# Six attention layers on one core: V leaves the projections, probabilities times tokens instead, masks and exps moved between engines, shifts by transfers

## The chip, the cores and the metric

One Trainium2 chip, one of its cores. The metric is the device time of one execution in microseconds. An execution is a single launch; all weights and inputs come from device memory and the result goes back to it. Five engines work beside each other, each with its own instruction queue in program order: TensorE (PE in the profile, PEld its weight loads), VectorE (DVE), ScalarE (ACT), GpSimd (POOL) and SyncE (SP, which issues the transfers here). They meet at semaphores only.

## The reference

The input x has 4 batches of 512 tokens of 128 numbers. Everything is float32. Two parts follow each other.

```
# part 1: attention with relative positions, 16 heads of 8, on layernorm(x)
score = ((q + u) @ k^T + relative_shift((q + v) @ pos^T)) / sqrt(8)
x1 = x + softmax(score) @ val @ Wo + bo
# part 2: x = layernorm(x1), then six layers, each
x' = shift_tokens(x)                 # second half of the features comes from the token before
q, k, v = split(x' @ Wqkv)           # 16 heads of 64
q, k = rotary(l2norm(q) * qs), rotary(l2norm(k) * ks)
# windows of 32 queries see the 64 keys of their own and the previous window, masked
x = x + softmax(8 q k^T, masked) @ v @ Wo
xn = layernorm(shift_tokens(x)) * g + b
a, gate = split(xn @ W1 + b1)
x = x + (a * gelu(gate)) @ W2 + b2
# at the end: x + x1
```

## The kernel before

**Part 1** (`relative_attention`, L817) runs through 128 rounds. Score rows go out to a scratch array in device memory and come back shifted by one; the transfers of this keep the memory busy. At its end, x is loaded once more (L963), POOL adds `bo` (L1194), and the block closes with a meeting of all engines.

**Part 2** (`local_layers`, L45) works on tiles of 128 tokens: 4 tiles are one batch and are called a group here, 16 tiles a layer, 96 tiles the whole. It begins with the last projection of part 1 for all four batches (L595 to L605) and their norm. Then each engine walks the same list of periods (`PERIODS`, L161), one tile per period. Several tiles are in flight: in period n, TensorE projects K and V of tile n and Q of tile n+1, turns (transposes) q and k of tile n-1, makes the scores of tile n-1, turns the probabilities of n-2, multiplies them with V for n-3 and projects the output of n-3 (the order by hand is L606 to L629; the others are L296 for POOL, L410 for ACT, L765 for DVE). An engine never looks ahead in its list, so one wait holds all that stands behind it.

Of one tile: two halves of 512 columns each make K, V or Q (L463). DVE multiplies q and k by the two rotary tables (`rotate`, L643, four instructions of 1024 numbers), ACT squares them (L317), DVE sums the squares by head (L652), POOL makes the inverse norms by three Newton steps for this tile (L243 to L266), adds the rotary halves (L240, four instructions) and scales q and k (L275). TensorE turns them (L473), ACT copies them out (L335, L344). The mask enters the scores as a bf16 matmul (L491); 64 small matmuls add q times k (L499). DVE takes the maximum (L658) and subtracts it (L666), ACT takes all exps in one instruction (L363), DVE sums, inverts and divides (L674, L681, L687), TensorE turns the probabilities (L510), ACT copies them (L369). SP spreads v over `vwin` by 16 transfers a tile (L177 to L189), 64 small matmuls make the head outputs (L529), ACT copies them (L376), 8 matmuls with Wo follow (L541), DVE adds to x (L694).

Once a group, after the fourth tile's addition: TensorE shifts the tokens by two matmuls with a shifted identity (`shift`, L545), DVE takes the statistics of the layernorm (L696), POOL the deviation (L277), ACT normalises in eight instructions of 64 numbers with a scale and a bias by partition (L393), TensorE turns (L561), three pairs of W1 matmuls (`hidden`, L569), three gelus on ACT (L402, with a table load before them and one before the next exp), three gates on DVE (L721), W2 (L579) and the addition (L730). PSUM (the matmuls' output memory) has eight banks; `ROOM` (L118) says which kind of result uses which, and `take` (L437) makes TensorE wait until the former user of a bank has been read.

## Time and profile before

| | us |
|---|---|
| three timed runs: median (lowest to highest) | 2131.49 (2127.36 to 2133.46) |
| the profiled execution, its own time | 2129.15 |
| its span in the profile | 2127.4 |
| part 1, until the meeting of the engines | about 442 |

| engine | busy share of the span |
|---|---|
| PE | 95% |
| POOL | 71% |
| DVE | 70% |
| ACT | 60% |

Busy shares are means over both parts. A row of the timeline gives the start and the length of a run of equal instructions; matmul passes overlap their neighbours by about 0.2 us of modelled drain, so the cost of a step is read from its start to the start of the next step. A float32 matmul shows as two passes, a transpose as one. In a row of waits or lines, "<-" names what ended the idle time. The granted clock of TensorE has two levels, shown as 1.00 (2.4 GHz) and 0.50 (1.2 GHz).

### The profile page before, as it was taken

To read this page: it belongs to the slowest core of one execution; us is meant where nothing else is said; L and a number is where in the kernel's file an instruction comes from. 1 tells how busy PE (TensorE), PEld (TensorE's weight loads), DVE (VectorE), ACT (ScalarE), POOL (GpSimd) and SP (SyncE) were. 2 spreads that over 40 slices of the span, in tenths; PEclk is the share of its full clock that TensorE was granted. 3 is DMA by queue.
4 is the path that set the end of the run, shared out by engine and by line. 5 is a ranking of instruction groups with operands and counts; after the bars stand their busy time and mean duration, and the time that the engine had idled before them with its cause. 6 is when DMAs were issued, how large, how long until landed. Compare 5 with 4: busy or idle time off the path is not lost.

```text
span 2127.4 us, 84221 instructions
## 1 busy us (share of the span) xinstructions
PE 2025.2 (95%) x35763; PEld 1357.7 (64%) x35763; DVE 1498.2 (70%) x2267; ACT 1285.3 (60%) x1844; POOL 1521.0 (71%) x2315
## 2 busy tenths in 40 slices
PE   6899998979999999999999999999999999999997
PEld 2555555545666667766676666766676666766665
DVE  3445454458877788778777788777787788777873
ACT  4676767535655666566655566566665666566653
POOL 4344444468888788777887788778887788877880
PEclk9999999989999999999999999999999999999998
DMA  6999999922224222242232322224222242222221
GB/s 201 331 347 354 340 352 351 328 73 59 65 67 115 63 66 70 62 114 62 63 73 63 111 68 66 63 64 112 67 72 64 61 118 62 67 63 63 66 70 41
DMA packets 121588, 261.51 MB, mean 123 GB/s; under 512 B 29140, under 2 KB 36224, under 8 KB 120448
## 3 DMA queue, kind: packets, MB, share of 16 engines
q1 hardware_dynamic: 121216, 256.13, 41.3%
q8 instruction: 285, 4.67, 0.9%
q14 instruction: 87, 0.71, 0.1%
HBM read 87.06 MB, written 68.29 MB: 73 GB/s over the span
## 4 chain that ended last, share of the span: by engine, by line
PE 72%; POOL 2%; DVE 2%; issue 1%; ACT 1%; POOLq 0%; DVEq 0%; ACTq 0%
PE ring L463 24%; PE ring L529 9%; PE ring L473 8%; PE yps L541 8%; PE ring L499 7%; PE ring L569 5%; PE ring L510 4%; PE tpose L579 3%; PE ring L491 1%; DVE turned L643 1%; PE tpose L551 1%; PE tpose L561 1%; POOL ropes L229 0%; POOL roped L275 0%; PE yps L454 0%
## 5 line engine op out<-in xcount | busy, mean ns | idle before, releaser
L643 DVE TENSOR_TENSOR turned<-ring,ropes 128x1024 f32<-128x1024 f32 x384 | 452.2, 1220 | 301.4 <-PE ring L463 301.4
L240 POOL TENSOR_TENSOR roped<-turned 128x512 f32<-128x512 f32 x384 | 522.1, 1385 | 171.8 <-PE ring L473 171.0
L463 PE MATMUL ring<-wqkv,xT 128*128 128x512 f32 x1152 | 565.2, 614 | 6.1 <-ACT xT L328 4.9
L275 POOL TENSOR_TENSOR roped<-roped,rnorm 128x1024 f32<-128x1024 f32 x192 | 361.2, 1902 | 7.5
L1188 POOL TENSOR_SCALAR less<-less,lowest 128x512 f32<-128x512 f32 x256 | 174.4, 692 | 216.1 <-DVE lowest L1141 216.1
L1141 DVE CUSTOM_DVE_ANT_0 less<-ps_b,shifted 128x512 f32<-128x512 f32 x256 | 166.7, 689 | 211.7 <-issue 89.5
L463 PEld LDWEIGHTS ring<-wqkv,xT 128*128 128x128 f32 x1152 | 197.6, 191 | 161.0 <-issue 149.3
L369 ACT COPY pT<-ring 128x1024 f32<-128x1024 f32 x96 | 97.1, 1012 | 305.3 <-PE ring L510 305.3
L529 PEld LDWEIGHTS ring<-pT,vwin 64*64 64x64 f32 x12288 | 198.3, 134 | 51.4 <-issue 51.1
L317 ACT ACTIVATE squares<-ring 128x1024 f32<-128x1024 f32 x192 | 197.2, 1027 | 55.0 <-DVE turned L643 54.9
L529 PE MATMUL ring<-pT,vwin 64*64 64x32 f32 x12288 | 219.4, 220 | 4.3 <-issue 2.6
L652 DVE TENSOR_REDUCE ss<-squares 128x16 f32<-128x1024 f32 x192 | 221.3, 1184 | 1.1 <-ACT squares L317 0.9
L473 PEld LDWEIGHTS ring<-ident,roped 128*128 128x128 f32 x1536 | 175.1, 142 | 72.1 <-issue 40.8
L473 PE MATMUL ring<-ident,roped 128*128 128x128 f32 x1536 | 205.4, 277 | 10.7 <-POOL roped L275 5.1
L499 PEld LDWEIGHTS ring<-kT,qT 64*32 64x32 f32 x12288 | 140.6, 105 | 98.3 <-issue 96.2
L541 PE MATMUL yps<-wo,oT 128*128 128x128 f32 x1536 | 187.4, 275 | 1.2 <-ACT oT L376 1.1
L972 PE MATMUL ps_b<-posm,qvT 32*128 32x512 f32 x512 | 147.1, 662 | 41.4 <-DVE lowest L1141 39.0
L541 PEld LDWEIGHTS yps<-wo,oT 128*128 128x128 f32 x1536 | 179.1, 192 | 1.6 <-ACT oT L376 1.6
L499 PE MATMUL ring<-kT,qT 64*32 64x64 f32 x12288 | 174.4, 224 | 2.3 <-issue 2.2
L1048 PEld LDWEIGHTS ps_b<-ident,less 128*128 128x128 f32 x1024 | 111.4, 142 | 93.6 <-POOL less L1188 76.9
L344 ACT COPY kT<-ring 128x1024 f32<-128x1024 f32 x96 | 97.0, 1011 | 101.7 <-PE ring L473 101.7
L1241 ACT ACTIVATE pT_a<-ps_b 128x512 f32<-128x512 f32 x256 | 141.5, 614 | 24.8 <-PE ps_b L1048 24.6
(134 smaller groups left out, 3242.0 us busy)
## 6 DMA issues: line engine op xcount, KB each, us to landing
vwin<-v SPq DMA_DIRECT2D x1536, 64.0 KB, 2.0
shifted<-scratch_w SPq DMA_DIRECT2D x64, 1024.0 KB, 12.0
scratch_w<-wrows SPq DMA_DIRECT2D x48, 1026.0 KB, 10.2
scratch_w<-x SPq DMA_DIRECT2D x16, 1026.0 KB, 9.9
wqkv<-in_l_wqkv SPq DMA_DIRECT2D x6, 1536.0 KB, 6.7
wo<-in_l_wo SPq DMA_DIRECT2D x6, 512.0 KB
w<-in_l_w SPq DMA_DIRECT2D x6, 342.0 KB
w<-in_l_w SPq DMA_DIRECT2D x6, 171.0 KB
```

The lines of the kernel that those rows point to most:

```text
L240: nc.gpsimd.tensor_tensor(halves[2][:, :, side, :], halves[0][:, :, side, :], halves[1][:, :, 1 - side, :], ALU.add).then_inc(s[name + "_a ...
L275: nc.gpsimd.tensor_tensor(whole, whole, norm, ALU.mult).then_inc(s[name + "_roped"], 1)
L317: nc.scalar.activation(squares[:, n, :], ring[:, room(name.upper()), :, :].rearrange("p b c -> p (b c)"), ACT.Square).then_inc(s[name + "_ ...
L463: last = nc.tensor.matmul(out[:, half, :], xT[:, t % SEQT * P:(t % SEQT + 1) * P], wqkv[:, layer_of(t), at + half * 512:at + (half + 1) * ...
L473: last = nc.tensor.transpose(out[:, j * P:(j + 1) * P], roped[:, n, j * P:(j + 1) * P], ident[:, :])
L499: last = nc.tensor.matmul(out[W * win:W * win + W, r, j * W2:(j + 1) * W2], qT[rows, j, W * win:W * win + W], kT[rows, j, at:at + W2], sta ...
L529: last = nc.tensor.matmul(out[a * DH:(a + 1) * DH, r, at:at + W], vwin[rows, p, win, j * DH:(j + 1) * DH], pT[rows, j, W * win:W * win + W ...
L541: last = nc.tensor.matmul(out[:, 0:D], oT[:, j % 2, j // 2, :], wo[:, layer_of(t), j, :], start=j == 0, stop=j == PAIRS - 1)
L643: ins = nc.vector.tensor_tensor(turned[:, n, part, :].rearrange("p (h d) -> p h d", d=DH), heads, table, ALU.mult)
L652: nc.vector.tensor_reduce(ss[:, n * HEADS:(n + 1) * HEADS], squares[:, n, :].rearrange("p (h d) -> p h d", d=DH), AX.X, ALU.add).then_inc( ...
L1141: nc.vector.tensor_tensor_reduce(less[:, c % 2, k, :], ps[:, 2 + k, :], shifted[:, c // 2 % NR, k, c % 2, :], -SCALE0, HIGHEST, ALU.add, A ...
L1188: nc.gpsimd.tensor_scalar(less[:, c % 2, k, :], less[:, c % 2, k, :], -1.0, lowest[:, c % 2, k:k + 1], ALU.mult, ALU.add).then_inc(s["scal ...
```

## The change

- V is no longer projected, copied, spread or multiplied. Instead x itself is laid out by SP in `xwin` (seven transfers a group), for each query window the 64 tokens that it may see, already shifted. TensorE multiplies these tokens by the probabilities of all 16 heads (`attend`: 8 matmuls of 32 rows, 128 columns and 512 moving columns, in four row groups and four banks), ACT copies the result by two instructions, and 16 matmuls with `wvo` give the output. `wvo` is Wv times Wo by head, made once a layer by 8 transposes and 16 matmuls.
- The mask is added by DVE as it reads the scores out (`take_scores`); the maximum is taken from that copy; q is no longer scaled by its norm, the exps take it as their scale, so they are 16 instructions of 64 numbers, one a head, each with a scale and a bias by partition.
- POOL divides the probabilities and does the Newton steps for two tiles at once; the scaling of q is gone. DVE turns the probabilities in blocks of 32 by 32 (`turn_p`) in place of TensorE and the ACT copy.
- The shift of the tokens before the second norm is done by two transfers into `xs` (`shift`, now SP's): one of 127 partitions, one of a single partition. DVE's `statistics` waits for both.
- All orders of the periods are new, with one more to two more tiles in flight; K and Q of one tile are projected in one period. FFN steps of a group sit in periods of their own: with n modulo 4, `statistics` and the W2 matmuls in 1, `turn_xn` in 2, two `hidden` at the end of 3, the third at the start of 0.
- In part 1, the output projection, the residual and the norm of batches 0 to 2 are done between the rounds (`FINISH`), x stays in its buffer, and the first layer's Wqkv is loaded before the block closes. Part 2 begins with batch 3's projection alone.

The core of the diff, new lines:

```diff
+        ROOM = {"AT": 3, "AP": 4, "XT": 3, "K": 2, "Q": 0, "QT": 1, "KT": 1, "S": 0, "O0": 1, "O1": 2, "Y": 4, "XN": 3, "H0": 0, "H1": 1, "H2": 2, "F": 3, "WV": 1, "M0": 1, "M1": 1}
...
+            def windows(g):
+                p, half = g % 2, D // 2
+                tiles = x[:, g % BATCH * SEQT:(g % BATCH + 1) * SEQT, :]
+                if g == BATCH - 1:
+                    sp.wait_ge(s["normed"], SEQT)
+                elif g >= BATCH:
+                    sp.wait_ge(s["x_done"], g - BATCH + 1)
+                at_least(sp, s["o_made"], SEQT * (g - 1))
+                low, high, up = slice(0, half), slice(half, D), W + 1
+                moves = [(xwin[:, p, :, 1, low], tiles[:, :, low]),
+                         (xwin[1:P, p, :, 1, high], tiles[0:P - 1, :, high]),
+                         (xwin[0:1, p, 1:SEQT, 1, high], tiles[P - 1:P, 0:SEQT - 1, high]),
+                         (xwin[W:P, p, :, 0, low], tiles[0:P - W, :, low]),
+                         (xwin[0:W, p, 1:SEQT, 0, low], tiles[P - W:P, 0:SEQT - 1, low]),
+                         (xwin[up:P, p, :, 0, high], tiles[0:P - up, :, high]),
+                         (xwin[0:up, p, 1:SEQT, 0, high], tiles[P - up:P, 0:SEQT - 1, high])]
+                for dst, src in moves:
+                    sp.dma_start(dst, src).then_inc(windows_in[p], 16)
+            def shift(g):
+                if lives(g):
+                    tiles = x[:, g % BATCH * SEQT:(g % BATCH + 1) * SEQT, D // 2:D]
+                    sp.wait_ge(s["y_added"], SEQT * (g + 1))
+                    at_least(sp, s["xn_made"], g)
+                    sp.dma_start(xs[1:P, :, :], tiles[0:P - 1, :, :]).then_inc(s["shifted"], 16)
+                    sp.dma_start(xs[0:1, 1:SEQT, :], tiles[P - 1:P, 0:SEQT - 1, :]).then_inc(s["shifted"], 16)
...
+            for g in range(GROUPS + 2):
+                if g < GROUPS:
+                    windows(g)
+                shift(g - 2)
+                if g % BATCH == 2 and g // BATCH + 1 < DEPTH:
+                    load_layer(g // BATCH + 1)
...
+                if live(t) and t % 2 == 0:
+                    m = t // 2
+                    sums, of_pair, part = (y.rearrange("p t h -> p (t h)") for y in (ss[:, m % 2, :, :], rnorm[:, m % 2, :, :],
+                                                                                      newton[:, :, :]))
+                    pool.wait_ge(s["q_summed"], t + 2)
+                    pool.wait_ge(s["k_summed"], t + 2)
...
+            def divide(t):
+                if live(t):
+                    pool.wait_ge(s["rinv_made"], t + 1)
+                    whole = probs[:, t % 2, :, :, :].rearrange("p r j k -> p (r j) k")
+                    nc.gpsimd.tensor_tensor(whole, whole, rinv[:, :, :].rearrange("p r j -> p (r j)").unsqueeze(2).broadcast_to(
+                        [P, HEADS, W2]), ALU.mult).then_inc(s["p_normed"], 1)
...
+                add_b2(group_of(n - 13))
+                add(1, n - 1)
+                divide(n - 4)
                 norms(n - 2)
...
+                    act.wait_ge(s["ebias_made"], t + 1)
+                    for r in range(2):
+                        for j in range(PAIRS):
+                            h = 2 * j + r
+                            of_head = probs[:, t % 2, r, j, :]
+                            ins = nc.scalar.activation(of_head, of_head, ACT.Exp, scale=norm_of(t)[:, h:h + 1],
+                                                       bias=ebias[:, t % 2, r, j:j + 1])
+                    ins.then_inc(s["exped"], 1)
+            def copy_o(t, half):
+                if live(t):
+                    act.wait_ge(s["o_made"], t + 1)
+                    at_least(act, s["y_made"], t - 1)
+                    nc.scalar.copy(xpT[:, t % 2, :, 2 * half:2 * half + 2, :].rearrange("p h w q -> p w h q"),
+                                   pair("O" + str(half)).rearrange("p w (h q) -> p w h q", q=W)
+                                   ).then_inc(s["o_copied" + str(half)], 1)
...
+                copy_xn(group_of(n - 11))
+                copy_q(n - 2)
+                copy_next_wvo(n - 2)
+                gelus(group_of(n - 12), 2)
+                gelus(group_of(n - 12), 1)
+                gelus(group_of(n - 12), 0)
+                exps(n - 3)
+                square(1, n)
+                copy_k(n - 2)
+                copy_x(n + 1)
                 square(0, n)
+                copy_o(n - 4, 0)
+                copy_o(n - 4, 1)
+                normalise(group_of(n - 9))
...
+            def attend(t):
+                if live(t):
+                    p = t // SEQT % 2
+                    pe.wait_ge(s["p_turned"], t + 1)
+                    pe.wait_ge(windows_in[p], WINDOWS * (t // SEQT // 2 + 1))
+                    take("O0", t)
+                    take("O1", t)
+                    for half in (1, 0):
+                        for win in range(WT):
+                            rows = slice(W * win, W * win + W)
+                            last = nc.tensor.matmul(pair("O" + str(win // 2))[:, win % 2, :], xwin[rows, p, t % SEQT, half, :],
+                                                    pT[rows, t % 2, :, half, :], start=half == 1, stop=half == 0)
+                    last.then_inc(s["o_made"], 1)
+            def project_out(t):
+                if live(t):
+                    for half in range(2):
+                        pe.wait_ge(s["o_copied" + str(half)], t + 1)
+                        pe.wait_ge(s["wvo_copied" + str(half)], t // (SEQT * BATCH) + 1)
+                    out = take("Y", t)
+                    for h in range(HEADS):
+                        last = nc.tensor.matmul(out[:, 0:D], xpT[:, t % 2, h, :, :].rearrange("p w q -> p (w q)"),
+                                                wvo[:, layer_of(t), h // PAIRS, h % PAIRS, :], start=h == 0,
+                                                stop=h == HEADS - 1)
+                    last.then_inc(s["y_made"], 1)
...
+                        at = 2 * INNER + j * P
+                        last = nc.tensor.transpose(out[:, j * P:(j + 1) * P], wqkv[layer % 2][:, at:at + P], ident[:, :])
...
+                            rows, at = slice(r * DH, (r + 1) * DH), a * PAIRS // 2 + j
+                            last = nc.tensor.matmul(out[:, r, j * D:(j + 1) * D], wvT[rows, at, :], wo[layer % 2][rows, at, :],
...
+                hidden(group_of(n - 12), 0)
+                turn_x(n + 1)
                 project("K", n)
+                project("Q", n)
+                turn_qk(1, n - 2)
+                project_out(n - 5)
+                attend(n - 4)
+                scores(n - 2, 0)
+                scores(n - 2, 1)
+                project_ffn(group_of(n - 13))
+                turn_xn(group_of(n - 10))
                 turn_qk(0, n - 1)
+                next_wvo(n - 1)
+                hidden(group_of(n - 11), 2)
+                hidden(group_of(n - 11), 1)
...
+                    seen = mask[:, 1 if t % SEQT == 0 else 0, :].unsqueeze(1).broadcast_to([P, HEADS, W2])
+                    nc.vector.scalar_tensor_tensor(probs[:, t % 2, :, :, :].rearrange("p r j k -> p (r j) k"),
+                                                   pair("S").rearrange("p r (j k) -> p (r j) k", k=W2), QK_SCALE, seen,
+                                                   ALU.mult, ALU.add).then_inc(s["scores_taken"], 1)
...
+                    nc.vector.scalar_tensor_tensor(ebias[:, t % 2, :, :], smax[:, :, :], -1.0, norm, ALU.mult, ALU.mult
+                                                   ).then_inc(s["ebias_made"], 1)
...
+            def turn_p(t):
+                if live(t):
+                    dve.wait_ge(s["p_normed"], t + 1)
+                    at_least(dve, s["o_made"], t - 1)
+                    nc.vector.transpose(pT[:, t % 2, :, :, :].rearrange("p h s q -> p (h s q)"),
+                                        probs[:, t % 2, :, :, :].rearrange("p r j k -> p (r j k)")).then_inc(s["p_turned"], 1)
...
-                    dve.wait_ge(s["shifted"], g + 1)
+                    dve.wait_ge(s["shifted"], 32 * (g + 1))
...
+                sum_squares(1, n - 1)
+                sum_squares(0, n - 1)
+                offsets(group_of(n - 10))
+                add_y(n - 6)
+                take_scores(n - 3)
+                take_max(n - 3)
+                exp_bias(n - 3)
+                gate(group_of(n - 12), 1)
+                add_ffn(group_of(n - 14))
+                gate(group_of(n - 12), 2)
+                statistics(group_of(n - 9))
+                turn_p(n - 4)
+                gate(group_of(n - 12), 0)
+                rotate(1, n)
                 rotate(0, n)
+                sum_probs(n - 3)
+                invert(n - 3)
+                if n == 8:
+                    first_norm()
...
+                    sp.wait_ge(s["c_taken"], 2 * 2 * ROUNDS // BATCH)
+                    sp.dma_start(kept["early"][:, 0:3 * INNER], layers["wqkv"][0]).then_inc(kept["qkv0_loaded"], 16)
...
+                        if c in FINISH:
+                            b = FINISH[c]
+                            pe.wait_ge(s["o_done"], max(turned_units, VARS * (b + 1)))
+                            for i in range(STEPS):
+                                last = nc.tensor.transpose(ps[:, 7, i * P:(i + 1) * P], attn[:, b * STEPS + i, :], ident[:, :])
+                            last.then_inc(s["a_turned"], 1)
...
+            FINISH = {85: 0, 93: 1, 101: 2}
```

## Rows read from the trace of the kernel before

**Rows 1.** The page, the chain that ended last (whole span)

```profile
PE ring L463 24%; PE ring L529 9%; PE ring L473 8%; PE yps L541 8%; PE ring L499 7%; PE ring L569 5%; PE ring L510 4%; PE tpose L579 3%; PE ring L491 1%; DVE turned L643 1%; PE tpose L551 1%; PE tpose L561 1%; POOL ropes L229 0%; POOL roped L275 0%; PE yps L454 0%
```

**Rows 2.** Busy time by windows, part 2: window, length, busy us by engine, clock, DMA

```profile
514.50:2053.80 1539.30, 1530.23 (x29817) 1056.11 (x29817) 1209.41 (x1469) 938.40 (x1217) 1244.89 (x1897) 1.00 0.29 74
```

**Rows 3.** Timeline of TensorE in two periods: start, length, what

```profile
1516.62 1.14 PE L529 MATMUL ring<-pT,vwin 64*64 64x32 f32 x64
1517.68 1.98 PE L463 MATMUL ring<-wqkv,xT 128*128 128x512 f32 x4
1519.60 0.41 PE L491 MATMUL ring<-bias,identb 32*32 32x512 bf16 x8
1519.94 0.96 PE L499 MATMUL ring<-kT,qT 64*32 64x64 f32 x64
...
1523.53 1.09 PE L510 MATMUL ring<-ident,probs 128*128 128x128 f32 x8
1524.46 0.60 PE L561 MATMUL tpose<-ident,xn 128*128 128x128 f32 x4
1524.90 1.95 PE L541 MATMUL yps<-wo,oT 128*128 128x128 f32 x16
1526.68 1.88 PE L463 MATMUL ring<-wqkv,xT 128*128 128x512 f32 x4
...
1529.53 5.31 PE L569 MATMUL ring<-xnT,w 128*114 128x512 f32 x12
...
1550.44 2.94 PE L579 MATMUL tpose<-w,hT 114*128 114x128 f32 x24
```

**Rows 4.** Timeline of TensorE in part 1, four row groups at once

```profile
23.08 1.31 PE L972 MATMUL ps_b<-posm,qvT 32*128 32x512 f32 x8
24.32 0.67 PE L990 MATMUL ps_b<-ident,x 128*128 128x128 f32 x4
```

**Rows 5.** Timeline of ACT, two of the eight instructions of normalise

```profile
1521.81 0.43 ACT L393 ACTIVATE xn<-x,offset,rstd 128x64 f32<-128x64 f32 x1
1522.14 0.39 ACT L393 ACTIVATE xn<-tpose,offset,rstd 128x64 f32<-128x64 f32 x1
```

**Rows 6.** Lines, 700 to 2100 us: busy us, mean ns | idle before

```profile
L240 POOL TENSOR_TENSOR roped<-turned 128x512 f32<-128x512 f32 x323 | 442.5, 1395 | 151.6 <-PE ring L473 151.5
L643 DVE TENSOR_TENSOR turned<-ring,ropes 128x1024 f32<-128x1024 f32 x320 | 377.0, 1220 | 256.5 <-PE ring L463 256.5
L275 POOL TENSOR_TENSOR roped<-roped,rnorm 128x1024 f32<-128x1024 f32 x162 | 304.8, 1902 | 6.3
...
L666 DVE TENSOR_TENSOR probs<-ring,smax 128x1024 f32<-128x1024 f32 x82 | 100.4, 1224 | 2.8
...
L344 ACT COPY kT<-ring 128x1024 f32<-128x1024 f32 x82 | 82.9, 1011 | 90.6 <-PE ring L473 90.6
...
L402 ACT ACTIVATE gelu<-ring,b 114x512 f32<-114x512 f32 x63 | 41.1, 685 | 9.2 <-PE ring L569 7.9 <-DVE hT L721 0.9
...
L402 ACT ACT_TABLE_LOAD x21 | 26.9, 1283 | 0.4
...
L701 DVE BATCH_NORM_STATS2 stats<-x 128x6 f32<-128x64 f32 x84 | 18.1, 216 | 13.4 <-PE tpose L553 13.4
```

**Rows 7.** Transfers, 700 to 2000 us: packets, MB, share of 16 engines; the vwin issues

```profile
q1 hardware_dynamic: 63141, 91.30, 28.0%
...
vwin<-v SPq DMA_DIRECT2D x1226, 64.0 KB, 2.0
```

**Rows 8.** Window at the end of a layer's load (its w2 and b1 have 114 partitions)

```profile
1196.50:1197.50 1.00, 0.79 (x51) 0.68 (x44) 1.00 (x2) 0.79 (x1) 1.00 (x1) 1.00 0.39 155
```

**Rows 9.** Windows at the end of the output's store (128 partitions)

```profile
2126.25:2126.50 0.25, 0.00 (x0) 0.00 (x0) 0.00 (x0) 0.00 (x0) 0.00 (x0) 0.50 0.95 270
2126.50:2126.75 0.25, 0.00 (x0) 0.00 (x0) 0.00 (x0) 0.00 (x0) 0.00 (x0) 0.50 0.11 29
```

**Rows 10.** Timeline of TensorE after a long wait, start of part 2

```profile
462.65 7.47 PE L463 MATMUL ring<-wqkv,xT 128*128 128x512 f32 x12 [4.93 <-ACT xT L328]
```

More of the change, by code:

```diff
@@ L556, in turn_xn, with next_wvo @@
+            def next_wvo(t):
+                step, layer = t % (SEQT * BATCH), t // (SEQT * BATCH) + 1
+                if t >= TURN_WV - SEQT * BATCH:
+                    if step == TURN_WV:
+                        turn_wv(layer)
+                    for a in range(2):
+                        if step == TURN_WV + 1 + a:
+                            make_wvo(layer, a)
             def turn_xn(g):
```

653 lines of the change are left out of this document (280 added, 373 removed).

## The prediction

> **What bounds the kernel now.** I read three views in this order. The chain of waits first [rows 1]: nearly every entry is TensorE, and only with lines of the second part. Then the busy time by windows [rows 2]: from the K projection of tile 4 (514.5 us) to that of tile 95 (2053.8 us) TensorE is busy 1530 of 1539 us, at full clock, so a period is TensorE's own sum. 91 periods in 1539.3 us are 16.92 us each, 67.7 us for a group of four. In that time DVE is busy 13.3 us a period (1209.41/91), ACT 10.3, POOL 13.7. Third the timeline of TensorE [rows 3], for what each step costs from its start to the next start: one of K, Q, V 1.92 us (1517.68 to 1519.60), the mask 0.34, the turn of the probabilities 0.93, the turn of xn 0.44, the output projection 1.78, half of the old attend 1.06 (1516.62 to 1517.68); the whole hidden about 5.4 and the W2 matmuls about 2.8, each its length less the drain. What holds for this kernel: microseconds taken from TensorE's list are gained as long as no other engine gets in its way. The reader is to see how thin the reserve of the others becomes.
>
> **TensorE's list.** Gone per tile: V 1.92, mask 0.34, turn of the probabilities 0.93, attend 2 x 1.06 = 2.12; together 5.31, or 21.2 a group, and the shift, 0.9 a group (1% of the span in the chain [rows 1] over 24 groups). Added per tile: eight more output matmuls, so 1.78 again, and the new attend. That one is not in this trace in its form, but its kind is: eight passes of 32 rows and 512 columns, on four row groups, take 1.24 us from start to start [rows 4], where passes of 128 rows take 0.48 each (1.92/4). Attend has sixteen such passes. Twice 1.24 is the high end with four abreast, half of the serial 16 x 0.48 = 7.7 is two abreast, 7.7 is none; the low end is 16/4 x 0.43 = 1.7. I take 2.2, near the row. So 4 x (1.78 + 2.2) = 15.9 a group. Wv times Wo is 8 transposes (0.93) and 32 half-height passes (between 1 and 4 us) a layer: 0.7 a group. Sum: 67.7 - 21.2 - 0.9 + 15.9 + 0.7 = 62.2 us a group, 15.5 a period.
>
> **ACT.** Two copies of 1.01 go (V, probabilities), one of 1.01 comes (attend's result in two halves) [rows 6]. The exps become 16 instructions of 64 numbers with scale and bias by partition. Normalise has that form: 0.33 us from start to start, 0.43 long [rows 5]. So 16 x 0.34 = 5.4 us, for 1.06 before; if they did not overlap, 6.9. ACT goes from 10.3 to 13.6 us a period, 15.1 at the worst: below TensorE's, but now long stretches of it are on the way to the next TensorE step. **DVE** keeps its sum: the division goes to POOL, the turn of the probabilities comes. It has no row; it moves 1024 numbers, for which rows of DVE give 1.22 [rows 6], a second pass would make 2.4; I take 1.2. The mask and the factor 8 ride on the copy that was there (1.22). **POOL** loses one scaling (1.90) and gains the division (1.90 by the same form [rows 6]); its fifteen small instructions now serve two tiles, which saves some 2 us a period. DVE stays near 13.3, POOL near 11.7, both under 15.5. Each can still be late once in a while; 0 to 1 us a group, taken as 0.
>
> **Where the order makes TensorE wait.** Each period has one loop that all engines share: scores of a tile done, then DVE's copy 1.22, maximum 1.2, bias 0.15; ACT's exps 5.4, square of k 0.92, copy of k 0.91; then TensorE may attend, since the copy of k frees attend's bank, and after it makes the next scores. With the hand-overs that is 10.1 us before attend. In the same time TensorE has turn q 0.93, x 0.12, K and Q 3.8, turn k 0.93, output 3.56: 9.3 us. By n modulo 4: in 1 it waits 10.1 - 9.3 = 0.8. In 2 the W2 matmuls of the period before make it 12.1: no wait. In 3, with turn_xn, 9.7: 0.4. In 0 the hidden matmuls make it 14.7; but the last of them ends at 6.4, then gelu 0.65, table load 1.28 [rows 6], exps, square and copy end at 15.8: 1.1. Together 2.3, so 64.5 us a group, 16.1 a period.
>
> **The new transfer.** This is the step that decides. TensorE's shift becomes two transfers, and DVE's `statistics` waits for them in the very period (n modulo 4 is 1) in which DVE adds the group's last y. Queued behind this wait on DVE are turn_p (attend needs it) and both rotates (ACT's square of k needs the first, so does the copy of k behind it in ACT's list). The addition is over about 0.9 us before the scores are done; DVE has 2.6 us of other work after that, so a landing up to 3.6 us after the addition costs nothing.
>
> How long does it take? It moves 127 partitions of 4 x 256 bytes, 130 KB. The 64 KB transfers of v land in 2.0 us [rows 7], and all transfers of this stretch ran at 91.30 MB / (0.28 x 16 x 1300 us) = 15.7 KB per us and DMA engine [rows 7]. Spread over 16 engines the shift would land after 2.0 + 0.3; on one engine after 2.0 - 0.3 + 8.3 = 10.0. Which is it? The load of a layer ends with a tail [rows 8]: for a whole microsecond only 39% of the DMA engines' time is used, while the store over 128 partitions ends within a quarter of a microsecond, from 95% to 11% [rows 9]. The load is the one case here with transfers of 114 partitions (w2, 171 KB, and b1), which is no multiple of 16: 155 KB moved in the tail at 39%, about what six engines would do that have all of w2 to themselves (6/16 = 0.375). So transfers over such a count use fewer engines, as many as divide it, and 127 has no divisor but 1. I take one engine: 10.0 us and 0.1 for SP's wake. The low end is 9.1 (the bulk of the store moves 270/16/0.95 = 17.8 KB per us and engine [rows 9], so 7.3 in place of 8.3), the high end 14 if pieces of 256 bytes cost more than their share.
>
> The Trainium skill states this outright, in "DMA: Bandwidth & Descriptors", section "Why a DMA increments its semaphore by 16 and not by 1": the number of engines is the largest up to 16 that divides the slowest dimension of both sides, and 127 partitions all go to one. The tail in the trace agrees with it for 114 (six engines). By the opposite reading, 16 engines, the sum would be the first rival's.
>
> Landing is then 10.1 - 0.9 = 9.2 us after the scores. Behind it: statistics 8 x 0.13 + 0.4 = 1.5 (overlapping, 0.22 each [rows 6]), turn_p 1.2, rotate k 2.3, square 0.92, copy 0.91: attend at 16.0 and not at 10.1, so 5.9 us more a group. In this wait TensorE stands idle for more than 6 us. After an idle 4.93 us at the start of part 2 twelve passes took 7.47 instead of 5.8 us [rows 10], since the clock was at its lower level. I add 2.1 for attend, scores and the W2 matmuls after it (between 0 and 4). 64.5 + 5.9 + 2.1 = 72.5 us a group, 18.1 a period. The windows' seven transfers have the same trouble (127, 95 and 33 partitions), but are issued some four periods ahead of their use, so they cost nothing.
>
> **Start and end.** Part 1 is bound by transfers and keeps its 442 us; the three finished batches lie in TensorE's gaps there. Part 2 starts with one batch and loaded weights, and its first periods lack the later steps: K of tile 5 comes some 20 us earlier (an estimate: five periods of about 11 us for five of 15 to 17). At the end, from K of tile 95 on, one more to two more periods drain, and one shift is bare: before 73.6 us (2127.4 less 2053.8), after about 92. Net -2 us (-10 without the slow transfer).
>
> **Sum.** 90 periods x (18.1 - 16.92) = +106, less 2: 2129 (the profiled execution's own time, 2 us over its span and 2 us under the median of the runs) + 104 = 2233 us.
>
> **Rivals.**
> First: the transfer is spread or otherwise in time (below 3.6 us). For it: the 64 KB transfers land in 2.0 us. Against it: the tail. Then 16.1 a period: 90 x (16.1 - 16.92) = -74, -10: 2045 us, faster. The point from which it decides is the landing: up to 3.6 us free, equal to the kernel before at about 7 us (3.2 us a group over 64.5, with little clock loss), slower beyond.
> Second: the transfer is in time, but the exps do not overlap (0.43 each, 1.5 us more in three of four periods, 4.5 a group): 17.25 a period, 2129 + 30 - 10 = 2149, slower by 1%. Against it: the eight of normalise overlap [rows 5].
> Third: attend runs two abreast (3.9 instead of 2.2, 6.8 a group) on top of the slow transfer; its wait then hides none of it: 90 x 1.7 more, 2386 us. Against it: [rows 4].
> That the change does less than it says: if the clock stays up after the wait and DVE catches up part of it, 68 to 70 a group: 2135 to 2180, the likeliest case's lower part.
>
> **How the numbers follow.** Likeliest 0.66, first rival 0.22, second 0.05, third 0.04, the rest 0.03. Time: 2233. The likeliest case's own range is 2130 to 2320 (landing 8 to 12 us, clock 0 to 4 us a group, loops +-1.5 us a group, which is +-34 us). The range over all takes in the first rival: 2030 to 2320. Within 0.3% of before (about 6 us, what a measurement can tell from nothing) lies little: 0.05. Faster: the first rival and the lowest part of the likeliest, 0.27. Slower: 0.68.
>
> **What would show it.** In the profile after: a landing of xs near 10 us; idle time of DVE before the statistics (bn_stats), released by that transfer, some 7 us x 24; rows of TensorE's attend with 16 passes in about 2.2 us; exps 0.34 us from start to start; a granted clock below 1.00 once a group; DMA share well under today's 0.29. If the transfer lands under 4 us, my step on its engines is wrong and the time is near 2045. If it lands at 10 and the kernel is still faster, the slack that I gave DVE before the statistics is wrong. If part 2 has 16.1 us or less in all other periods, the sums of the engines were right.

## The result and the profile after

The changed kernel takes 2238.27 us (median; 2234.71 to 2242.56), the kernel before 2132.47 beside it: ratio 1.0497, 95% interval 1.0464 to 1.0531. It is slower by 106 us. The profiled execution has a span of 2232.9 us.

The page after, part 1 (busy time) and part 4 (the chain that ended last, by engine and line):

```profile
PE 1887.8 (85%) x24771; PEld 1270.8 (57%) x24771; DVE 1523.8 (68%) x2363; ACT 1610.8 (72%) x3204; POOL 1305.9 (58%) x1639
...
ACT 26%; PE 26%; DVE 9%; DMA 9%; issue 8%; POOL 1%; SPq 1%; ACTq 0%; DVEq 0%; POOLq 0%
```

The chain of before is nearly all TensorE [rows 1]. Now TensorE and ACT have a quarter each, and 9% of the span, 200 us, is one kind of transfer. The busy time by windows, from K of tile 5 to K of tile 95, as [rows 2]:

```profile
526.40:2125.60 1599.20, 1374.15 (x19136) 957.21 (x19135) 1223.59 (x1548) 1231.38 (x2478) 1034.36 (x1245) 0.96 0.08 19
```

TensorE is busy 1374 of 1599 us: 15.3 us in a period of 17.77. Its list did get shorter (16.8 before), and 2.5 us a period of waiting have come in. The DMA share fell from 0.29 to 0.08, the clock from 1.00 to 0.96. The next fences show one group around its last addition of y. DVE:

```profile
1516.01 0.28 DVE L743 TENSOR_TENSOR x<-yps,x 128x128 f32<-128x128 f32 x1
1517.05 1.23 DVE L697 SCALAR_TENSOR_TENSOR probs<-ring,mask 128x1024 f32<-128x1024 f32 x1 [0.76 <-PE ring L539]
1518.31 1.22 DVE L704 TENSOR_REDUCE smax<-probs 128x16 f32<-128x1024 f32 x1
1519.56 1.14 DVE L715 SCALAR_TENSOR_TENSOR ebias<-smax,rnorm 128x16 f32<-128x16 f32 x1
1525.60 0.23 DVE L750 BATCH_NORM_STATS2 stats<-x 128x6 f32<-128x64 f32 x1 [4.90 <-DMA xs<-x]
```

SP's queue in the same stretch, the two issues of the shift:

```profile
1516.32 0.70 SPq L224 DMA_DIRECT2D xs<-x  x1
1517.07 6.50 SPq L225 DMA_DIRECT2D xs<-x  x1
```

The addition ends at 1516.29, the statistics start at 1525.60: the shift lands after 9.3 us. Windows while it runs (length, busy us by engine, clock, DMA share, GB/s):

```profile
1519.00:1520.00 1.00, 0.77 (x13) 0.80 (x15) 0.97 (x2) 0.08 (x1) 1.00 (x2) 1.00 0.08 17
1521.00:1522.00 1.00, 1.00 (x4) 0.49 (x3) 0.00 (x0) 1.00 (x3) 0.00 (x0) 1.00 0.08 18
```

A share of 0.08 of the DMA engines' time is used, at 17 to 18 GB/s. The rate is that of one engine in [rows 9] (17.8 KB per us), and kernel 5 below, with 122 partitions, has twice the share and nearly twice the rate: one engine carries the 127 KB. The divisor rule that the prediction took from [rows 8] holds here. What waits behind it, on ACT and then TensorE:

```profile
1530.55 1.02 ACT L357 ACTIVATE squares<-ring 128x1024 f32<-128x1024 f32 x1 [3.81 <-DVE turned L678]
1531.47 1.01 ACT L383 COPY kT<-ring 128x1024 f32<-128x1024 f32 x1
```

```profile
1513.60 2.00 PE L556 MATMUL ring<-pT,xwin 32*128 32x512 f32 x16 [0.72 <-ACT kT L383]
1515.53 1.48 PE L539 MATMUL ring<-kT,qT 64*32 64x64 f32 x128
...
1524.79 3.74 PE L568 MATMUL yps<-wvo,xpT 128*128 128x128 f32 x32
1532.73 3.51 PE L556 MATMUL ring<-pT,xwin 32*128 32x512 f32 x16 [4.20 <-ACT kT L383]
```

Follow the chain by its start times: the statistics start behind the landing at 1525.60, DVE's rotate of K ends about 1530.5, ACT squares and copies, TensorE attends at 1532.73. The same attend takes 2.00 us at 1513.60 and 3.51 after the wait; the windows say why (clock is the number before the DMA share):

```profile
1532.80:1536.10 3.30, 3.30 (x16) 1.21 (x16) 3.27 (x4) 1.14 (x2) 2.55 (x2) 0.54 0.01 2
1536.30:1537.50 1.20, 1.20 (x128) 1.19 (x123) 0.36 (x3) 1.20 (x2) 0.78 (x3) 1.00 0.00 0
```

After 4.2 us idle the granted clock is 0.54, near its lower level (1.2 GHz), as in [rows 10], where it is 0.50 from 462.7 to 466 us; for the scores it is back at 1.00. The sums over the run, from the waits (total, times, longest):

```profile
PE ring L556 <- ACT kT L383: 177.7, 91, 8.8
...
DVE stats L750 <- DMA xs<-x: 120.4, 24, 9.3
```

### The profile page after: what moved, and what is told of

The parts are those of the page before. It is cut to its first block, busy times and chain, and to the rows that moved or that the text cites. A ratio compares the mean times of both kernels' runs of the same rounds, so it can differ in the third digit from the quotient of the medians.

```text
span 2232.9 us, 61471 instructions
## 1 busy us (share of the span) xinstructions
PE 1887.8 (85%) x24771; PEld 1270.8 (57%) x24771; DVE 1523.8 (68%) x2363; ACT 1610.8 (72%) x3204; POOL 1305.9 (58%) x1639
## 4 chain that ended last, share of the span: by engine, by line
ACT 26%; PE 26%; DVE 9%; DMA 9%; issue 8%; POOL 1%; SPq 1%; ACTq 0%; DVEq 0%; POOLq 0%
ACT probs L394 15%; DMA xs<-x 9%; PE ring L556 8%; PE ring L618 6%; PE ring L539 5%; ACT kT L383 4%; DVE turned L678 3%; PE tpose L629 3%; ACT squares L357 3%; PE ring L522 2%; ACT qT L374 1%; DVE probs L697 1%; DVE smax L704 1%; ACT L394 1%; DVE stats L750 1%
## 5 line engine op out<-in xcount | busy, mean ns | idle before, releaser
L394 ACT ACTIVATE probs<-probs,ebias,rnorm 128x64 f32<-128x64 f32 x1536 | 519.7, 428 | 41.9 <-DVE ebias L715 41.5
L556 PE MATMUL ring<-pT,xwin 32*128 32x512 f32 x1536 | 232.7, 726 | 181.8 <-ACT kT L383 177.7
L568 PE MATMUL yps<-wvo,xpT 128*128 128x128 f32 x3072 | 358.8, 275 | 1.6 <-DVE x L743 1.6
L568 PEld LDWEIGHTS yps<-wvo,xpT 128*128 128x128 f32 x3072 | 350.7, 192 | 2.3 <-issue 2.3
L277 POOL TENSOR_TENSOR roped_k<-turned 128x512 f32<-128x512 f32 x192 | 240.2, 1274 | 186.9 <-DVE turned L678 100.9
L277 POOL TENSOR_TENSOR roped_q<-turned 128x512 f32<-128x512 f32 x192 | 239.5, 1270 | 77.7 <-PE ring L522 77.7
L403 ACT COPY xpT<-ring 128x1024 f32<-128x1024 f32 x192 | 185.1, 1016 | 126.9 <-PE ring L556 126.9
L319 POOL TENSOR_TENSOR probs<-probs,rinv 128x1024 f32<-128x1024 f32 x96 | 182.6, 1902 | 125.3 <-DVE rinv L729 125.3
L313 POOL TENSOR_TENSOR roped_k<-roped_k,rnorm 128x1024 f32<-128x1024 f32 x96 | 183.1, 1907 | 3.8
L509 PE MATMUL ring<-wqkv,xT 128*128 128x512 f32 x384 | 175.2, 599 | 5.9 <-DVE gelu L768 5.9
L539 PE MATMUL ring<-kT,qT 64*32 64x64 f32 x12288 | 154.3, 237 | 22.5 <-issue 14.3
```

Of the source, the lines that this page charges most:

```text
L277: nc.gpsimd.tensor_tensor(halves[2][:, :, side, :], halves[0][:, :, side, :], halves[1][:, :, 1 - side, :], ALU.add).then_inc(s[name + "_a ...
L313: nc.gpsimd.tensor_tensor(whole, whole, norm, ALU.mult).then_inc(s["k_roped"], 1)
L319: nc.gpsimd.tensor_tensor(whole, whole, rinv[:, :, :].rearrange("p r j -> p (r j)").unsqueeze(2).broadcast_to([P, HEADS, W2]), ALU.mult).t ...
L394: ins = nc.scalar.activation(of_head, of_head, ACT.Exp, scale=norm_of(t)[:, h:h + 1], bias=ebias[:, t % 2, r, j:j + 1])
L403: nc.scalar.copy(xpT[:, t % 2, :, 2 * half:2 * half + 2, :].rearrange("p h w q -> p w h q"), pair("O" + str(half)).rearrange("p w (h q) -> ...
L509: last = nc.tensor.matmul(out[:, half, :], xT[:, t % SEQT * P:(t % SEQT + 1) * P], wqkv[layer_of(t)][:, at + half * 512:at + (half + 1) * ...
```

## The experiments

All times are medians (kernel 9 has a single execution); ratios are to the kernel before on the same chip, with their 95% intervals. For each kernel the time is cut at two marks of TensorE's timeline, K of tile 5 and K of tile 95; these 90 periods are "a period", the rest up to the end of the span is "tail". "n1" is the mean distance from the start of one scores block to the next where the later one lies in a period with n modulo 4 = 1, the period in which the shift is awaited (21 of them, n = 13 to 93). There is no kernel 8.

```
kernel                          time     K(5) at  period   tail   n1
before                          2132     529.2    16.94    73.6   -
after                           2238     526.4    17.77   107.3   20.9
1  shift in 112+15              2123     528.9    16.44   102.2   15.2
2  windows cut, shift whole     2251     534.3    17.82   108.9   20.9
3  both cut                     2117     529.4    16.50   102.7   15.5
4  statistics late, shift whole 2191     534.6    17.14   110.4   15.4
5  shift in 122+5               2151     532.3    16.77   105.2   16.6
6  3, one exp (prices its form) 2037     528.5    15.67    94.2   14.3
7  3, exps split in two         2192     533.2    17.32    97.3   16.9
10 7, square of Q ahead too       2318     533.7    18.62   103.7   18.4
9  3, attend by window          2119     531.9    16.45   104.7   15.5
11 3, norm by DVE, no maximum   2049     527.3    15.77    94.5   14.1
12 11, all transfers whole      2179     530.5    17.19   100.7   20.5
```

**1. The shift cut at 112 partitions** (seven times 16, and 15). Theory A: the one-engine transfer. Rival B: something else in the new loop. Code is shortened in all edits shown: the increments and the counts of the waits, which follow the number of transfers, are left out.

```
-  sp.dma_start(xs[1:P, :, :], tiles[0:P - 1, :, :])
+  sp.dma_start(xs[1:113, :, :], tiles[0:112, :, :])
+  sp.dma_start(xs[113:P, :, :], tiles[112:P - 1, :, :])
```

> The changed kernel with its token shift of 127 partitions cut into two transfers, of 112 and of 15 partitions; all else as it is. Theory A (one DMA engine carries all of the 127 partitions, DVE's statistics wait for it and hold turn_p and the rotates): the landing falls from 9.3 us after the addition to about 2.5 to 3.5 us, the wait of the statistics (120 us in all) goes to under 10 us, and with the clock's drop behind it 6 to 7.5 us a group go: 2055 to 2095 us, ratio to before 0.965 to 0.98. Theory B (the loop over scores, sixteen exps and attend is the bound, the transfer only fills a wait that is there anyway): at most 20 us less than 2238.

Measured 2122.94, ratio 0.9945 (0.9925 to 0.9965). 115 us come back, and the kernel is 0.5% faster than before. DVE's wait for xs is gone from the periods: it reaches the statistics 4.3 us after the addition, and the data lie there. (In kernels 7 and 10 it is there sooner and waits until 3.4 us after the addition: that is the landing of 112 + 15.) SP's second issue, 6.50 us with the whole shift, now takes 0.86 (timeline of SP):

```profile
1381.58 0.65 SPq L224 DMA_DIRECT2D xs<-x  x1
1382.28 0.86 SPq L225 DMA_DIRECT2D xs<-x  x1
1383.19 0.72 SPq L226 DMA_DIRECT2D xs<-x  x1
```

B, which allowed 20 us, is out as the main cause of the loss. But A had 2055 to 2095: more was left besides the transfer than I worked out, and what it was stands in the section on the prediction.

**2. The windows' transfers cut, the shift whole**, and **3. both cut.** C: TensorE's stray stops come from the seven slow window transfers.

```
-  (xwin[1:P, p, :, 1, high], tiles[0:P - 1, :, high]),
+  (xwin[1:113, p, :, 1, high], tiles[0:112, :, high]),
+  (xwin[113:P, p, :, 1, high], tiles[112:P - 1, :, high]),
   (the same for the pieces of 95 and 33 partitions: 80 + 15, 32 + 1)
```

> The changed kernel with only the seven window transfers cut so that no part of more than one partition has a count with few divisors (127 into 112 and 15, 95 into 80 and 15, 33 into 32 and 1); the shift stays whole. Theory A says that the windows are ahead of their use: the time stays within 10 us of 2238. Theory C (TensorE's own instructions arrive by the same DMA engines, and the scores stop for 1.8 us a group while the windows crowd one engine): that stop goes, 40 to 70 us less, 2170 to 2195.

> Both cuts at once. Theory A alone: as the shift's cut alone, 2055 to 2095. A and C together: some 45 us less than that, 2010 to 2050; the prediction's first rival gave 2045.

Measured 2250.7 (1.0562, 1.0532 to 1.0592) and 2116.68 (0.9931, 0.9908 to 0.9954). C falls. Alone, cutting the windows costs some 12 us, little over the 10 that A allowed. Of the 14 us between the two traces 8 lie before K of tile 5, where kernel 4, whose windows are whole, is as late; what they come from is not shown. With the shift cut the intervals of kernels 1 and 3 overlap. As the prediction said, the slowness of these transfers costs nothing: no gain comes from cutting them.

**4. The statistics moved behind the inversion in DVE's period**, transfers whole: the turn of the probabilities and the rotates no longer stand behind the wait.

```
                 statistics(group_of(n - 9))     (taken out before turn_p)
                 ...
                 invert(n - 3)
+                statistics(group_of(n - 9))
```

> The changed kernel with the slow transfer kept, but DVE's statistics moved behind the rotates, the sum and the inverse of the same period, so that nothing of that period stands behind the wait. Theory A: DVE waits little, attend is on time; 5 to 7 us a group go, 2070 to 2120 us. A rival (the wait only moves to ACT's normalise and to the copy of q behind it): 1 to 3 us a group go, 2165 to 2215. Theory B: no change.

Measured 2190.56, ratio 1.0274 (1.0257 to 1.0292): the time that the rival gave, but not by its way. n1 is 15.4, as with the cut transfer, but the period with n modulo 4 = 2 went from 16.4 to 19.1. From the waits of this kernel:

```profile
POOL rstd L326 <- DVE meanvar L754: 230.2, 24, 27.1
DVE turned L678 <- POOL roped_q L277: 103.0, 26, 7.2
...
PE ring L522 <- POOL roped_k L313: 58.1, 25, 5.8
```

The first is 175.8 us in the kernel after, the second 16.4. The third is 8.5. POOL's small `deviations` stands in its list ahead of the additions and the scaling of K of the next period. The wait was handed in good part from DVE's queue to POOL's. ACT's normalise, to which the rival had it move, waited once in the whole run, 15.7 us, as in the kernel after. The move cured 48 of 115 us.

**5. The shift cut at 122 partitions** (two times 61, and 5): two engines.

> The shift is cut at 122 partitions (2 times 61) and 5, so that by the rule of divisors two DMA engines move the large part and five the small one. Theory (the landing after the addition decides, and the engines are counted by divisors): the transfer takes about 2 + 7.5/2 = 5.7 us instead of 9.25. That is some 2 us over the 3.6 us that DVE has free, so 1.5 to 2.5 us a group are lost against the kernel with 112 + 15 (2122.9): 2140 to 2185. Rival (any cut does, since what costs is that one transfer sits alone on its queue): as the kernel with 112 + 15, 2118 to 2130. Second rival (the divisor rule is wrong and 122 partitions take the same time as 127): within 10 us of 2238.

Measured 2150.75, ratio 1.0081 (1.0055 to 1.0108), inside the range of the theory. The addition ends at 1400.11:

```profile
1400.89 2.81 SPq L225 DMA_DIRECT2D xs<-x  x1
```

```profile
1406.23 0.23 DVE L751 BATCH_NORM_STATS2 stats<-x 128x6 f32<-128x64 f32 x1 [2.67 <-DMA xs<-x]
```

That is 6.1 us after the addition (5.8 in the median of the 24), with this share while it runs (as above, the last but one number):

```profile
1402.00:1402.50 0.50, 0.00 (x0) 0.00 (x0) 0.47 (x2) 0.00 (x0) 0.00 (x0) 1.00 0.15 32
```

0.15 at 32 GB/s is about twice the 0.08 at 17 of the whole shift: two engines for one. So landings of 9.3, 5.8 and 3.4 us, the first two met by DVE waiting, give n1 = 20.9, 16.6 and 15.2: it is the landing, by engines, and not that a lone transfer sits on the queue.

**6. Kernel 3 with one exp instruction** over 1024 numbers.

```
-  for r in range(2):
-      for j in range(PAIRS):
-          h = 2 * j + r
-          ... activation(of_head, of_head, Exp, scale=norm[:, h], bias=ebias[:, r, j])
+  activation(flat, flat, Exp, scale=norm[:, 0:1], bias=ebias[:, 0, 0:1])
```

> Both transfers spread, and ACT's exps are one instruction over all 1024 numbers instead of 16 of 64: each head's own norm and maximum are left out (head 0's stand for all), so that it prices the exps' form alone. Theory (with the transfers in time the loop scores, maximum, exps, square, copy of k, attend is what still holds TensorE over its own sum): exps 1.06 instead of 5.42, the loop is 4.3 us shorter, all waits of TensorE for the copy of k go, and it falls from 2116.7 to 2030 to 2075. Rival (what is left over TensorE's sum is not this loop but POOL's additions and the wvo periods): 2095 to 2120.

It leaves out each head's own norm and maximum. Measured 2036.54, ratio 0.9548 (0.9511 to 0.9586): the exps' form costs 80 us. A group is 62.7 us (4 x 15.67). That looks like TensorE's list, which the prediction had at 62.2, but it is not the list alone. The 90 periods of kernel 1 and of this kernel:

```profile
528.90:2008.70 1479.80, 1348.00 (x19136) 948.61 (x19135) 1220.60 (x1547) 1229.01 (x2478) 1035.24 (x1245) 0.99 0.08 21
528.50:1939.00 1410.50, 1331.99 (x19135) 938.42 (x19134) 1206.14 (x1547) 864.28 (x1128) 1036.14 (x1246) 1.00 0.09 22
```

At a clock of 1.00 TensorE is busy 1332 us here, 59.2 a group; 3.5 us a group are waits even in this kernel.

**7. Kernel 3 with 8 exps, then square and copy of K, then the other 8.** An attempt to take the exps out of the way to attend and keep them.

```
   exps(n - 3, 0)
   square(1, n)
   copy_k(n - 2)
+  exps(n - 3, 1)
   copy_x(n + 1)
   square(0, n)
```

> Both transfers spread, nothing left out; ACT does 8 of the 16 exps, then the square and the copy of k that free TensorE's attend, then the other 8. The loop to attend is 2.7 us shorter while ACT's own sum is the same. Theory (the loop is what holds TensorE): as far as 2.7 us of the 4.3 suffice, the waits for the copy of k go in the periods without FFN: 2050 to 2090. Rival 1 (not the loop): 2105 to 2125. Rival 2 (the wait moves to DVE: the row sums start 1.8 us later, so POOL's division and the turn of the probabilities come late for the next attend): 2120 to 2160.

Measured 2192.33, ratio 1.0281 (1.0244 to 1.0318), slower than every theory said. In its waits:

```profile
DVE rsum L728 <- ACT probs L399: 210.2, 96, 6.2
...
PE ring L546 <- ACT squares L361: 100.2, 89, 6.0
...
PE ring L563 <- ACT kT L387: 39.3, 18, 2.5
```

The wait for the copy of K fell (79.4 us in kernel 3), but a new one of 100 us came: the scores' bank is that of Q and is freed by the square of Q, which I had left behind the second half of the exps. So it was run once more as **10**, with the second half behind the square of Q:

> Both transfers spread, nothing left out. ACT does 8 exps, the square of k, the copy of k, the copies of x and the square of q, and only then the other 8 exps. In the kernel with the exps split just around square and copy of k (2192) TensorE's wait for the copy of k fell to 39 us, but its scores waited 100 us for ACT's square of q, which frees the scores' bank and stood behind the second half of the exps. Theory (that square alone made it slow, and the loop of exps is what holds TensorE): both waits are gone, the periods come near those of the kernel with one exp instruction (15.7 us a period), 2035 to 2080. Rival (the row sums, the division and the turn of the probabilities, now later, hold attend): 2100 to 2160.

Measured 2318.34, ratio 1.0885 (1.0861 to 1.0908). My theory fell. The waits of this kernel:

```profile
DVE rsum L728 <- ACT probs L399: 368.0, 96, 6.8
ACT squares L361 <- DVE turned L685: 188.6, 133, 6.4
```

The end of the exps releases two ways, not one. The first is ACT's copy of K, then attend. The second is DVE's row sums, and behind these stand, in DVE's list, the sums of squares, the addition of y and the next scores' copy, maximum and bias, which the next exps need. From the first to the last of them the 16 exps take 5.4 us in kernel 3, 8.4 in kernel 7 and 10.6 in kernel 10, and the wait of the row sums grows with it. The theory had looked at one way only; kernels 6 and 11 shorten both.

**9. Kernel 3 with attend's matmuls window by window.**

```
-  for half in (1, 0):
-      for win in range(WT):
+  for win in range(WT):
+      for half in (1, 0):
```

> Both transfers spread; attend's matmuls are issued window by window, both halves of one window one behind the other, instead of one half over all four windows. Each accumulation then follows its own row group at once. If the four row groups run abreast whatever the order, attend stays at 1.93 us from start to start and the time at 2117. If only neighbours of different groups in the queue overlap, attend takes 3.9 us or more, 2 us a tile, of which the waits for the copy of k hide none: 2117 + 90 x 2 = 2300 or so.

Measured 2118.91 in a single execution beside 2116.68; TensorE's attend:

```profile
1515.99 2.02 PE L560 MATMUL ring<-pT,xwin 32*128 32x512 f32 x16 [0.73 <-ACT kT L387]
1517.94 1.48 PE L543 MATMUL ring<-kT,qT 64*32 64x64 f32 x128
```

1.95 us from start to start for 1.93: four row groups run abreast in either order. The third rival of the prediction is out, and the order of issue does not bring it in.

**11. Kernel 3 with the norm of Q multiplied on DVE** in place of maximum and bias, and one exp (removed lines in short).

```
-  take_max; ebias = -smax * norm; 16 x Exp(scale=norm, bias=ebias)
+  nc.vector.tensor_tensor(of_tile, of_tile, norm, ALU.mult)
+  nc.scalar.activation(flat, flat, ACT.Exp)
```

> Both transfers spread. In place of the maximum (1.22) and the bias (0.15 to 1.1), DVE multiplies the masked scores by the norms of q, one instruction of 1024 numbers, and ACT's exps are one instruction with no scale and bias. It leaves out the subtraction of the maximum and nothing else. Theory (the exps' length holds two loops: copy of k to attend, and row sums on DVE to the next scores): both are 4.3 us shorter, as in the kernel with one exp for all heads (2036.5), and DVE has one small instruction less: 2020 to 2045. Rival (the multiplication costs DVE a slower pass, 2.3 us in place of 1.2, since it reads a broadcast operand): 2050 to 2090.

Measured 2048.75, ratio 0.9619 (0.9594 to 0.9643): faster than both kernels, by 82 and by 189 us, and 4 us above my range. The multiplication takes 1.44 us in the mean, not 1.22; what the trace shows of this stands in the last section. Its softmax does without the subtraction of the maximum, which holds only while the scores are small enough for exp; a kernel for other inputs would have to bound them.

**12. Kernel 11 with all transfers whole.**

> The kernel with the norms multiplied on DVE and one exp instruction (2048.8; it leaves out the subtraction of the maximum), but with all transfers whole again, as in the change. The loops are 4.3 us shorter than in the change, so this asks whether slack would have hidden the one-engine transfer. Theory (nothing hides it: DVE has only some 3 us of work between the addition of y and the statistics, however short the exps are, and the landing of 9.3 us moves everything behind it): attend of the period after each shift about 4.5 us later than with the cut transfer, 1.5 us more by the lower clock, 24 times: 2048.8 + 110 to 150, 2160 to 2200. Rival (the shorter exps give back what the transfer takes): 2070 to 2120.

Measured 2179.29, ratio 1.0241 (1.0206 to 1.0277): 130.5 us for the whole transfers, against 121.6 in the kernels with the long exps (after less kernel 3). Slack elsewhere hides none of it. n1 grows by 6.4 us here and by 5.4 there, but the 9 us between the two totals are within their intervals; that a shorter loop pays more is not shown.

## Why the prediction held, and what in it did not

The forecast of 2233 us, slower by the one-engine transfer, was borne out in sign and cause: cutting the shift alone gives 115 us back. That it came within 5 us is luck, since five terms of its sum were off and cancel each other. They are worth going through.

**TensorE's list: 62.2 us a group predicted, 59.2 measured** (kernel 6, clock 1.00). The list was 3 us too long. Attend takes 1.93 from start to start, where 2.2 was taken from [rows 4], which is 1.1 of it. The scores, taken over unchanged, come in one run of 128 passes and take 5.8 us a group for 6.7 before; K and Q take 14.0, where before two of the three projections took 14.9. The other engines came out as summed: ACT 13.7 us a period (1231/90; 13.6 predicted), DVE 13.6 (13.3), POOL 11.5 (11.7).

**The transfer's engines and landing: right.** One engine, 9.3 us after the addition, where the sum had 10.1 and its low end 9.1. That low end came from the 17.8 KB per us and engine at the end of the store [rows 9], and the windows show 17 to 18. The average over the stretch [rows 7], 15.7, was too low for this transfer; why is not shown. The Trainium skill, in "DMA: Bandwidth & Descriptors", section "Why a DMA increments its semaphore by 16 and not by 1", gives the divisor rule; shares of 0.08 for 127 partitions and 0.15 for 122 agree with it.

**What the landing costs: 8.0 us a group predicted, 5.3 measured.** By the table the group is 71.1 us with the transfer whole and 65.8 with it cut. DVE's wait was to be 6.5 us (landing 10.1, of which 3.6 free); it is 5.0 (120.4/24). The landing is 0.8 earlier, and DVE comes to the statistics 0.7 later, 4.3 us after the addition in kernel 1, mainly since the bias before them takes 1.14 us there and not 0.15. Behind the wait, I had attend 10.1 us after the scores without the transfer; in kernel 3 the scores end at 1522.10 and attend starts at 1533.46, 11.4 later. With the transfer it was at 16.0 by the prediction, and is at 15.7 (1517.0 to 1532.73). So the transfer adds 4.3, not 5.9. The lower clock adds 26 us of TensorE's busy time over 90 periods (1374 against 1348 in kernel 1), 1.2 a group by 22.5 groups, not 2.1: in the rows shown attend alone is slowed, not the scores behind it.

**The other waits: 2.3 us a group predicted, 5.9 measured** (kernel 1, 1480 less 1348 us over 22.5 groups). This step failed too. The wait for the copy of K, the only one in the sum, is 3.4 us a group. Its loop is longer than summed (the bias was taken at 0.15 us and is 0.47 in the mean, up to 1.73), and TensorE's own list, which hides part of the loop, is shorter. The rest, 2.4 us a group, was taken as nothing: waits for ACT's copies around `next_wvo` 0.8, stops with no releaser in the trace 0.9, waits for the gates 0.5, for POOL and others 0.2. List and waits are off by 3.0 and 3.6 us in opposite directions (0.7 more is TensorE's busy time in kernel 1 over kernel 6, with clocks of 0.99 and 1.00), so 65.8 looks close to the predicted 64.5. The exps themselves are as predicted: 16 in 5.4 us, from [rows 5].

**Start and end: -2 us predicted, +31 measured.** This step of the prediction failed most. At the start I had K of tile 5 some 20 us earlier; it is 2.8. (Kernels 1 to 12 have it at 527 to 535, the kernel after at 526, though little in front of it differs; so some 8 us of this vary from kernel to kernel.) From TensorE's timeline in kernel 3, the first lines of part 2:

```profile
451.25 1.91 PE L583 MATMUL ring<-ident,early 128*128 128x128 f32 x8
455.93 1.51 PE L595 MATMUL ring<-early,wvT 64*128 64x128 f32 x16 [2.77 <-DMA early<-in_l_wo]
458.63 2.08 PE L595 MATMUL ring<-early,wvT 64*128 64x128 f32 x16 [1.19 <-ACT wvo L424]
...
487.14 1.84 PE L526 MATMUL ring<-ident,roped_k 128*128 128x128 f32 x8 [4.76 <-POOL roped_k L317]
493.22 2.05 PE L543 MATMUL ring<-kT,qT 64*32 64x64 f32 x128 [4.24 <-ACT squares L361]
```

The first product of Wv and Wo stands, with a wait for Wo's load, ahead of the first projection. In the kernel after that projection starts at 459.9, where the kernel before starts its own at 454.0: 6 us later. Part 1 is 2.3 us of this (TensorE starts part 2 at 444.4 for 442.1), against the prediction, which left it as it was. The five periods from there to K of tile 5 were to take 11 us each and take 13.3, with waits as in these rows and a clock of 0.73 from 442 to 529 us (0.86 before). I had counted the product in every layer's sum and forgotten the first, which nothing overlaps. At the end, from K of tile 95 on, 107.3 us where 92 was predicted. The windows of this stretch, after and before:

```profile
2125.60:2232.90 107.30, 75.93 (x822) 52.91 (x820) 41.58 (x76) 55.70 (x113) 29.01 (x33) 0.89 0.05 13
2053.80:2127.40 73.60, 54.62 (x1002) 39.97 (x1000) 30.23 (x60) 31.09 (x44) 20.47 (x28) 0.90 0.20 50
```

TensorE's work behind K of tile 95 alone grew by 21 us, more than the 18 that I had for everything, and its waits by 12, from 19.0 to 31.4. With the transfers cut they are 26.2 (kernel 3) and with one exp 19.1 (kernel 6): 5 us are the bare last shift, 7 the form of the exps. Two of its last waits, timeline of TensorE after:

```profile
2166.11 2.68 PE L556 MATMUL ring<-pT,xwin 32*128 32x512 f32 x16 [2.33 <-ACT kT L383]
...
2213.85 1.12 PE L610 MATMUL tpose<-ident,xn 128*128 128x128 f32 x4 [12.99 <-ACT xn L448]
```

**The sum.** Periods: +106 predicted; +75 measured (90 x (17.77 - 16.94)). Start and end: -2 and +31. Together +104 predicted and +106 measured. The periods were put 31 us too high and the two ends 33 too low. The agreement of the totals to 2 us is luck; that of the mechanism is not.

**The rivals.** The first (transfer in time) was given 2045 us; kernel 1, which makes it true, has 2123. Of the 78 us between, the table puts (16.44 - 16.1) x 90 = 31 in the periods and 38 in start and end (+28 for -10); the rest is that its profiled execution was a little quicker than its median. So with the transfer in time the kernel is faster than before by 0.5%, not by 4%. The point from which the transfer decides lies lower too: the group before has 67.7 us, only 1.9 over 65.8 and not 3.2 over 64.5. The second (exps that do not overlap) is out: 0.34 us from one to the next.

## What to carry to other kernels

Ahead of any DMA that an in-order engine waits for, look at its partition count: here 127 cut into 112 and 15 took DVE's wait out of the periods and gave 115 us back. Compare a sum of an engine's steps with its busy time in the windows, not with a period that has waits in it: here the period of kernel 6 agreed with the forecast list, and the list was 3 us a group shorter. When work is moved to an idle engine, follow the end of each long instruction group down every queue that it releases (here ACT's and DVE's), since shortening one way by lengthening another gave less than half in kernel 4 and lost in kernels 7 and 10. Sum the first and the last periods by themselves: here they held 33 us that the forecast did not have.

## What the runs showed of the hardware

- The bias, a DVE instruction of 128x16 numbers with two SBUF inputs, takes 0.17 to 1.73 us. In the kernel after, each of the 44 (of 96) that took over 0.3 us ends within 0.12 us of the end of a POOL instruction with two SBUF inputs. After, DVE and then POOL:

```profile
1573.99 1.70 DVE L715 SCALAR_TENSOR_TENSOR ebias<-smax,rnorm 128x16 f32<-128x16 f32 x1
```

```profile
1573.75 1.90 POOL L313 TENSOR_TENSOR roped_k<-roped_k,rnorm 128x1024 f32<-128x1024 f32 x1
```

  They end at 1575.69 and 1575.65. The scores' copy, which reads PSUM and one SBUF tensor, keeps its 1.22 us. In kernel 11 the multiplication (two SBUF inputs) takes 1.23 us alone and 2.13 beside POOL's two additions, which themselves take 3.48 in place of 2.50. The Trainium skill, in "GPSIMD Engine Reference", section "1. Specifications", names this contention for DVE instructions with two SBUF inputs; the rows agree, and show that a small DVE instruction can last until the end of POOL's.
- The issue of a small transfer right behind a one-engine transfer held SP for 6.50 us, behind a two-engine one for 2.81, behind one over 16 engines for 0.86.
- DVE's transpose of 128x1024 fp32 numbers in blocks of 32 takes 1.22 us in the mean, as the scores' copy and the maximum do.
- TensorE's scores stop in the periods with no releaser that the trace shows: 8 times in the kernel after (12.7 us in all, up to 1.8), 10 times in kernel 3 (13.6 us), 4 times in kernel 6 (3.7 us). Cutting the windows did not take them away. Their cause stays open.
